# Attention one: the ring of products as two double banks in place of four banks, its reads 1024 columns wide, the layer norm's statistics in four parts

## The chip, the cores and the metric

The kernel runs on one core of a Trainium2 chip. The metric is the device time of the whole program in microseconds, lower is better. Time before: 3014.7 us, the median of 3 runs (3010.32 to 3017.59).

## The reference, cut to what matters

The program is a small language model tower of two layers on 8 sequences of 1024 tokens and width 256. The change touches the first attention only:

```python
h = W.T[tokens]                                   # (8, 1024, 256)
xh = layernorm(h).reshape(b, c, 16, 16).transpose(0, 2, 1, 3)
qkv = einsum('bhce,ef->bhcf', xh, Wqkv) + bqkv    # 16 heads of 16
q, k, v = split(qkv, 3, axis=-1)
att = einsum('bhqe,bhke->bhqk', q, k) / sqrt(16)
att = softmax(att * tril(ones((c, c)), k=-1))     # masked scores are 0, not -inf
out = einsum('bhqk,bhke->bhqe', att, v)
h = h + out.transpose(0, 2, 1, 3).reshape(b, c, d) @ Wr + br
```

A masked score counts as 0 in the softmax, so each row also needs a sum of later values of V (the suffix sums), scaled by the row's maximum.

## The kernel before, in words

**Units of work.** A sequence has 8 tiles of 128 tokens. A half (hb, 16 in all) is one sequence with 8 of its 16 heads; a group is 4 heads, so a half has two groups and the program 32. The code works in windows, one a group. A window issues 36 score slots (`S`): each fills one of 3 score banks in PSUM with 512 columns of K times Q, ACT turns it into exponentials (L554), POOL masks the diagonal blocks (L476), and PE sums them with V into `pv` in six bursts (`PV`, L717).

**The other work.** `window()` (L146) lays every other job at a slot of the window, from the positions in `AT` (L137). All engines walk the same list of events in the same order, each doing its part, with semaphores between them. gi = 0 is the window with the prologue of the next half (statistics, normalising, transposes, Q, K, V), gi = 1 the one without. `sections` runs "init" (prologue alone, then maxima), "first" (the two windows of half 0), a hardware loop over 14 halves ("loop"), "last" and "final". In the positions of `ALONE` a job has no scores beside it.

**The ring.** All products except scores and `pv` share the banks of `ring`, four of 512 fp32 columns. Each use takes the next bank; before it PE waits in `bank_free` (L338) until the use four before was read. The uses are: `XT`, transposes of the normalised tiles, read by ACT; `QK`, the products Q and K in halves of 512 tokens, read twice by ACT (L571, L572), then split into three bf16 parts by POOL and ACT (L488, L580, L493); `V`, read by DVE; `SUF`, the suffix sums; `PT`, transposes of `pv`; `OT` and `WR`, the output projection; `MX`, the scores of the next group with a mask, of which DVE takes maxima (L643); and `CT`, a transpose of 32 columns of the maxima, which a DMA carries into the stack that scores read. PE fills the two MX banks of a pair of heads together and DVE reads them one by one. The two uses of `MX` of a step are 18 steps a window, spread from slot 1 or 2 to 32.

**The layer norm.** `LN_STATS` (slot 1 of gi = 0) makes the statistics of all 8 tiles on DVE (L611, L615), `LN_NORM` (slot 3) has POOL compute (variance + eps) to the power -0.5 (L482, L484) and DVE normalise all 8 tiles (L620). MX uses are at slots 2 and 3, in this order on DVE:

```python
at(pos_of["LN_STATS"], ("LN_STATS",))
at(pos_of["LN_NORM"], ("LN_NORM",))
at(pos_of["XT"], ("R", "XT", "act", 0), ("R", "XT", "act", 1))
```

## Time and profile before

| | us |
|---|---|
| profiled execution, in all | 3005.22 |
| its span | 3002.8 |
| median of the runs | 3014.7 |
| PE busy | 2581.3 (86%) |
| DVE busy | 2118.6 (71%) |
| ACT busy | 1523.5 (51%) |
| POOL busy | 1640.4 (55%) |

The span is what the profiler recorded from the first to the last instruction. The first attention is its first half, to about 1520 us; the rest is experts, second attention and feed-forward. PE is the tensor engine's matmuls, PEld its weight loads beside them, DVE the vector engine, ACT the scalar engine, POOL GpSimd. "ring<-Km,Qm" means that an instruction writes the tile `ring` and reads `Km` and `Qm`. A bracket with an arrow gives the idle time of an engine before an instruction and whose instruction ended it. The granted clock of the tensor engine has mean 0.928 over the span, as a share of 2.4 GHz.

### The profile page before, as it was taken

Reading aid. Unit: us, or ns where it says so; the run is one execution under the profiler, and the core shown is the slowest. Engines: PE = TensorE matmul, PEld = TensorE weight load, DVE = VectorE, ACT = ScalarE, POOL = GpSimd, SP = SyncE. Lnnn points to the kernel's source line nnn. Section 1 sums busy time; section 2 is a strip of 40 time slices with the busy share of each in tenths; the row PEclk is TensorE's granted clock in tenths of the full one; section 3 lists DMA queues with packets and bytes.
Section 4 is the critical chain, followed back from the end, with each engine's and each line's share of the span. In section 5 each row is a group of like instructions: output and inputs, shape, how many; then the busy total and the mean of one; then the engine's idle time right before and its main releaser. Section 6 shows DMA issues by size and latency. Waiting matters only on the chain. (4 is left out here: it accounts for less than half of the span.)

```text
span 3002.8 us, 58475 instructions
## 1 busy us (share of the span) xinstructions
PE 2581.3 (86%) x15254; PEld 1510.3 (50%) x15318; DVE 2118.6 (71%) x5668; ACT 1523.5 (51%) x3246; POOL 1640.4 (55%) x2564
## 2 busy tenths in 40 slices
PE   1778988888988888888868999898998979999999
PEld 0323433333333333343345666666666647666666
DVE  2657766777766767676567999898888965556554
ACT  1345555555555655555513655555555634444444
POOL 3664343333334333334245877777776757777675
PEclk7679999999999999999969999999999979999999
DMA  3353343344343344334230000000000000000000
GB/s 56 89 116 62 52 63 54 52 70 69 51 63 56 53 59 70 58 54 63 36 137 1 1 1 1 1 1 1 1 1 1 1 3 16 16 14 16 16 16 18
DMA packets 81300, 113.27 MB, mean 38 GB/s; under 512 B 25100, under 2 KB 37144, under 8 KB 80536
## 3 DMA queue, kind: packets, MB, share of 16 engines
q1 hardware_dynamic: 76360, 101.44, 19.8%
q0 software_dynamic: 3072, 8.39, 1.0%
q10 hardware_dynamic: 1744, 2.16, 0.2%
q14 instruction: 92, 0.75, 0.1%
q8 instruction: 32, 0.52, 0.1%
HBM read 18.98 MB, written 8.39 MB: 9 GB/s over the span
## 5 line engine op out<-in xcount | busy, mean ns | idle before, releaser
L554 ACT ACTIVATE probs<-scoresT 128x512 f32<-128x512 f32 x1152 | 639.7, 604 | 632.4 <-PE scoresT L697 622.9
L643 DVE TENSOR_REDUCE cand<-ring 128x4 f32<-128x512 f32 x1152 | 724.1, 680 | 219.6 <-PE ring L753 167.3
L476 POOL TENSOR_SCALAR_AFFINE_SELECT probs<-probs 128x256 f32<-128x256 f32 x512 | 204.9, 414 | 468.5 <-ACT probs L554 462.4
L697 PE MATMUL scoresT<-stage 98*128 98x512 bf16 (+3 forms) x1536 | 410.3, 344 | 22.2 <-ACT probs L554 16.6
L753 PE MATMUL ring<-Km,Qm 64*128 64x512 bf16 (+2 forms) x1792 | 253.0, 321 | 160.5 <-DVE cand L643 130.5
L717 PE MATMUL pv<-probs,Vg 128*32 128x512 f32 (+3 forms) x3072 | 325.2, 545 | 28.3 <-POOL probs L476 25.9
L753 PEld LDWEIGHTS ring<-Km,Qm 64*128 64x128 bf16 x1792 | 83.5, 95 | 375.6 <-DVE cand L643 239.5
L1180 PE MATMUL mm<-w_W,hT 128*128 128x256 f32 x1024 | 259.1, 399 | 8.7 <-ACT z L1268 2.8
L1200 PE MATMUL mm<-w_W,x2T 128*128 128x512 f32 x512 | 242.4, 596 | 0.3 <-DVE x L1419 0.2
L697 PEld LDWEIGHTS scoresT<-stage 98*128 98x128 bf16 x1536 | 114.5, 99 | 234.4 <-issue 139.1
L1261 ACT ACTIVATE hT<-mmT,w_be,w_g 128x128 f32<-128x128 f32 x512 | 185.5, 469 | 90.7 <-PE mmT L1191 90.7
L1180 PEld LDWEIGHTS mm<-w_W,hT 128*128 128x128 f32 x1024 | 207.1, 202 | 36.4 <-issue 0.3
L1622 PE MATMUL down_ps<-q_down,turned 128*128 128x256 f32 (+1 forms) x768 | 201.5, 396 | 2.3 <-ACT turned L1652 2.3
L1676 POOL TENSOR_TENSOR val<-val,power 128x960 f32<-128x960 f32 (+2 forms) x68 | 129.0, 1898 | 113.0 <-ACT power L1663 113.0
L717 PEld LDWEIGHTS pv<-probs,Vg 128*32 128x32 f32 x3072 | 85.5, 115 | 191.9 <-issue 154.7
L1584 PE MATMUL gate<-q_w_gate,turned 128*128 128x352 f32 x512 | 174.0, 462 | 0.7 <-ACT turned L1647 0.5
L1584 PE MATMUL up<-q_w_up,turned 128*128 128x352 f32 x512 | 173.0, 460 | 0.0
L1622 PEld LDWEIGHTS down_ps<-q_down,turned 128*128 128x128 f32 (+1 forms) x768 | 134.9, 189 | 68.2 <-issue 43.4
L1635 ACT ACTIVATE act_g<-gate 128x352 f32<-128x352 f32 x128 | 59.3, 463 | 208.9 <-PE gate L1584 202.5
L1328 POOL TENSOR_TENSOR u<-z,w_g 128x512 f32<-128x512 f32 x128 | 160.2, 1272 | 1.7 <-ACT z L1268 1.7
L1268 ACT ACTIVATE z<-mm,nmw,rw 128x256 f32<-128x256 f32 x256 | 124.0, 571 | 48.1 <-POOL nmw L1345 47.8
L1200 PEld LDWEIGHTS mm<-w_W,x2T 128*128 128x128 f32 x512 | 98.2, 192 | 87.5 <-issue 83.3
(254 smaller groups left out, 5280.9 us busy)
## 6 DMA issues: line engine op xcount, KB each, us to landing
stage<-parts SPq DMA_DIRECT2D x256, 96.0 KB, 2.8
stage<-parts SPq DMA_DIRECT2D x256, 64.0 KB, 2.8
Qm<-parts SPq DMA_DIRECT2D x128, 128.0 KB, 2.6
Km<-parts SPq DMA_DIRECT2D x128, 128.0 KB, 2.7
stage<-parts SPq DMA_DIRECT2D x256, 32.0 KB, 2.4
out<-result SPq DMA_DIRECT2D x64, 128.0 KB, 1.7
stage<-ct SPq DMA_DIRECT2D x128, 4.0 KB
w_W<-in_W SPq DMA_DIRECT2D x4, 512.0 KB
```

The lines of the kernel that those rows point to most:

```text
L476: nc.gpsimd.affine_select(out=d, in_=d, compare_op=ALU.is_gt, fill=0.0, base=0, pattern=[[0, 2], [1, P]], channel_multiplier=-1).then_inc( ...
L554: nc.scalar.activation(probs[:, buffer(slot), :], scoresT[slot % SCORE_BANKS][:], ACT.Exp, scale=SOFT).then_inc(exp_ok, 1)
L643: ins = nc.vector.tensor_reduce(c, src[:].rearrange("p (t a b) -> p t a b", t=c.shape[1], b=P), AX.X, ALU.max)
L697: ins = nc.tensor.matmul(scoresT[slot % SCORE_BANKS][:, at:at + hi - lo], Ks[0:ROWS, gi, hh, P * kt:P * kt + P], Qs[0:ROWS, gi, hh, lo:hi] ...
L717: ins = nc.tensor.matmul(pv[32 * hh:32 * hh + 32, lo:512], Vg[:, par, kt, hh, :], probs[:, buffer(slot), column:column + 512 - lo], start= ...
L753: ins = nc.tensor.matmul(out[x][:, P * at:P * (at + n)], Qm[half[x], hh // 2, P * i:P * i + P], Km[half[x], hh // 2, P * j:P * (j + n)], s ...
L1180: ins = nc.tensor.matmul(o, hT[:, 2 * e + c, :], w["W2"][:, c, e, :], start=False, stop=(e % 2 == 1 and c == 1))
L1200: ins = nc.tensor.matmul(mm1[p][:], x2T[same][:, c, :], w["W1"][:, c, 2 * p:2 * p + 2, :].rearrange("p e n -> p (e n)"), start=False, stop ...
L1261: nc.scalar.activation(hT[:, j, :], mmT[p][:, P * k:P * k + P], ACT.Relu, bias=w["be1"][:, j:j + 1], scale=w["g1"][:, j:j + 1]).then_inc(h ...
L1328: nc.gpsimd.tensor_tensor(u[same][:, 2 * p:2 * p + 2, :], z[same][:, 2 * p:2 * p + 2, :], w["g2"][:].rearrange("p (e n) -> p e n", e=E4)[: ...
L1584: ins = nc.tensor.matmul(out[:, 0:HALF], turned[par][:, 5 + c, :], wt[:, c, HALF * a:HALF * a + HALF], start=(c == 0), stop=(c == 1))
L1622: ins = nc.tensor.matmul(down[:, 0:D], turned[1 - u][0:rows, at, :], w["down"][0:rows, k, :], start=(n == 0), stop=(n == CHUNKS - 1))
```

## The change

The ring has two double banks of 1024 columns in place of four of 512, and each use fills one whole and is read by one instruction: both heads of an MX pair, all 8 tiles of `XT`, `V`, `SUF`, `PT` and `OT`, 1024 tokens of Q or of K, 4 tiles of `WR`. The buffer `f32part` is one of 1024 columns in place of two of 512. The statistics are made in four parts at slots 0, 2, 4 and 6, POOL's power is an event of its own (`LN_POWER`, slot 6), and the normalising has four parts at slots 10 to 13. `XT` moves from slot 7 to 14, `QK` from (11, 13, 18, 20) to (16, 22), `V` from 21 to 24, `OT` from 24 to 26, `PT` from 5 and 7 to 7, `RSUM` from 5 to 3, `SUF` from 12 to 9, `WR` from slots 1 and 2 of gi = 1 to 2 and 8, and the first MX of gi = 0 from slot 2 to 1. The diff, cut to its core (the parts left out are the same steps in the waits' counts and in SP's and POOL's code):

```diff
-SCORE_BANKS, RING_BANKS = 3, 4
+SCORE_BANKS, RING_BANKS = 3, 2
 PROBS = 16
+LN_PARTS = 4
+LN_TILES = TPB // LN_PARTS
...
 AT = {
-    0: {"LN_STATS": 1, "LN_NORM": 3, "XT": 7, "PV_COPY": 4, "EQ": 6, "TMP": 0, "PT": 5, "OT": 24, "WR": 25, "RSUM": 5, "SUF": 12, "QK": (11, 13, 18, 20), "MID_LAG": 2, "V": 21, "VG": 5, "LOAD": 0, "MX": 2, "MX_END": 32, "MX_CURVE": 1.0, "PV_HALF": 14},
-    1: {"PV_COPY": 4, "EQ": 6, "TMP": 0, "PT": 5, "WR": 1, "V": 8, "VG": 6, "LOAD": 0, "MX": 1, "MX_END": 32, "MX_CURVE": 1.0, "PV_HALF": 14},
+    0: {"LN_STATS": (0, 2, 4, 6), "LN_NORM": (10, 11, 12, 13), "XT": 14, "PV_COPY": 4, "EQ": 6, "TMP": 0, "PT": 7, "OT": 26, "WR": 27, "RSUM": 3, "SUF": 9, "QK": (16, 22), "MID_LAG": 2, "V": 24, "VG": 5, "LOAD": 0, "MX": 1, "MX_END": 32, "MX_CURVE": 1.0, "PV_HALF": 14},
+    1: {"PV_COPY": 4, "EQ": 6, "TMP": 0, "PT": 7, "WR": 2, "V": 8, "VG": 6, "LOAD": 0, "MX": 1, "MX_END": 32, "MX_CURVE": 1.0, "PV_HALF": 14},
     "V_IN": 0, "WR_IN": 1,
 }
-ALONE = {"LN_STATS": 0, "LN_NORM": 1, "XT": 2, "QK": (8, 9, 10, 11), "MID_LAG": 1, "V": 12, "PV_COPY": 1, "TMP": 2, "PT": 5, "OT": 11,
+ALONE = {"LN_STATS": (0, 0, 0, 0), "LN_NORM": (1, 1, 1, 1), "XT": 2, "QK": (8, 10), "MID_LAG": 1, "V": 12, "PV_COPY": 1, "TMP": 2, "PT": 5, "OT": 11,
          "WR": 14, "VG": 14, "LOAD": 14, "MX": 15, "MX_END": 35, "MX_CURVE": 1.0}
...
 
     if prologue:
-        at(pos_of["LN_STATS"], ("LN_STATS",))
-        at(pos_of["LN_NORM"], ("LN_NORM",))
-        at(pos_of["XT"], ("R", "XT", "act", 0), ("R", "XT", "act", 1))
+        for n in range(LN_PARTS):
+            at(pos_of["LN_STATS"][n], ("LN_STATS", n))
+            at(pos_of["LN_NORM"][n], ("LN_NORM", n))
+        at(pos_of["LN_STATS"][-1], ("LN_POWER",))
+        at(pos_of["XT"], ("R", "XT", "act"))
     if tail:
         at(0, ("PV", -1, 4))
         at(3 if scores else 0, ("PV", -1, 5))
         at(pos_of["PV_COPY"], ("PV_COPY", -1, 1))
         at(pos_of["TMP"], ("TMP", -1))
-        at(pos_of["PT"], ("R", "PT", "dve", -1, 0))
-        at(pos_of["PT"] + 2, ("R", "PT", "dve", -1, 1), ("OM", -1))
+        at(pos_of["PT"], ("R", "PT", "dve", -1), ("OM", -1))
     if ot:
-        at(pos_of["OT"], ("R", "OT", "act", 0), ("R", "OT", "act", 1))
+        at(pos_of["OT"], ("R", "OT", "act"))
     if wr:
-        for j in range(4):
-            at(pos_of["WR"] + (j // 2 if scores else 0), ("R", "WR", "dve", j))
+        for j in range(2):
+            at(pos_of["WR"] + (6 * j if scores else 0), ("R", "WR", "dve", j))
     if gi == 0 and scores:
         at(pos_of["RSUM"], ("RSUM",))
-        at(pos_of["SUF"], ("R", "SUF", "dve", 0), ("R", "SUF", "dve", 1))
+        at(pos_of["SUF"], ("R", "SUF", "dve"))
     if prologue:
-        for n in range(4):
-            at(pos_of["QK"][n], ("R", "QK", "act", n // 2, n % 2))
-            at(pos_of["QK"][n] + pos_of["MID_LAG"], ("MID", n // 2, n % 2))
+        for w in range(2):
+            at(pos_of["QK"][w], ("R", "QK", "act", w))
+            at(pos_of["QK"][w] + pos_of["MID_LAG"], ("MID", w))
     if v:
-        at(pos_of["V"], ("R", "V", "dve", 0), ("R", "V", "dve", 1))
+        at(pos_of["V"], ("R", "V", "dve"))
     if following:
...
-                uses.append([("R", "MX", "dve", 2 * p, k), ("R", "MX", "dve", 2 * p + 1, k)])
+                uses.append([("R", "MX", "dve", p, k)])
...
-        f32part = sb("f32part", [P, 2, 512])
+        f32part = sb("f32part", [P, S])
...
-        ring = [ctx.enter_context(nc.psum_tensor(f"ring{i}", [P, 512], F32)) for i in range(RING_BANKS)]
+        ring = [ctx.enter_context(nc.psum_tensor(f"ring{i}", [P, S], F32)) for i in range(RING_BANKS)]
...
-                        elif kind == "LN_NORM":
-                            wait_apart(pool, (mv_ok, hb + 2))
+                        elif kind == "LN_POWER":
+                            wait_apart(pool, (mv_ok, LN_PARTS * (hb + 2)))
                             nc.gpsimd.tensor_scalar(rstd[:], mv[:, :, 1], EPS, None, ALU.add).then_inc(rs_c, 1)
                             pool.wait_ge(rs_c, hb + 2)
                             nc.gpsimd.tensor_tensor(rstd[:], rstd[:], minus_half[:], ALU.pow).then_inc(rstd_ok, 1)
                         elif kind == "R" and e[2] == "QK":
-                            w, c = e[4:6]
+                            w = e[4]
                             read(pool, section, num, e)
-                            nc.gpsimd.tensor_tensor(f32part[:, c, :], f32part[:, c, :],
-                                                    parts[:, w, 0, 512 * c:512 * c + 512], ALU.subtract).then_inc(rest_ok, 1)
+                            nc.gpsimd.tensor_tensor(f32part[:], f32part[:], parts[:, w, 0, :], ALU.subtract).then_inc(rest_ok, 1)
                         elif kind == "MID":
-                            w, c = e[2:4]
-                            pool.wait_ge(mid_ok, 4 * (hb + 1) + 2 * w + c + 1)
-                            nc.gpsimd.tensor_tensor(parts[:, w, 2, 512 * c:512 * c + 512], f32part[:, c, :],
-                                                    parts[:, w, 1, 512 * c:512 * c + 512], ALU.subtract).then_inc(parts_ok, 1)
+                            w = e[2]
+                            pool.wait_ge(mid_ok, 2 * (hb + 1) + w + 1)
+                            nc.gpsimd.tensor_tensor(parts[:, w, 2, :], f32part[:], parts[:, w, 1, :], ALU.subtract).then_inc(parts_ok, 1)
...
                             elif e[2] == "QK":
-                                w, c = e[4:6]
...
-                                    act.wait_ge(w_in, 16 * WEIGHTS)
-                                    for s in (k_in if w else q_in):
-                                        wait(act, s, 16 * 12 * (hb + 1))
-                                    for s in max_in:
-                                        wait(act, s, 16 * 4 * 2 * (hb + 1))
-                                wait(act, parts_ok, 4 * (hb + 1) + 2 * w + c - 1)
-                                nc.scalar.activation(f32part[:, c, :], src[:], ACT.Identity, bias=b_q[:, w:w + 1])
-                                nc.scalar.activation(parts[:, w, 0, 512 * c:512 * c + 512], src[:], ACT.Identity,
+                                w = e[4]
+                                act.wait_ge(w_in, 16 * WEIGHTS)
+                                for s in (k_in if w else q_in):
+                                    wait(act, s, 16 * 12 * (hb + 1))
+                                for s in max_in:
+                                    wait(act, s, 16 * 4 * 2 * (hb + 1))
+                                wait(act, parts_ok, 2 * (hb + 1) + w)
+                                nc.scalar.activation(f32part[:], src[:], ACT.Identity, bias=b_q[:, w:w + 1])
+                                nc.scalar.activation(parts[:, w, 0, :], src[:], ACT.Identity,
                                                      bias=b_q[:, w:w + 1]).then_inc(read_act, 1)
...
+                            for t in part:
                                 ins = nc.vector.bn_stats(st[:, t, :], h[:, TPB * (hn // 2) + t, :])
                             ins.then_inc(stats_c, 1)
-                            wait_apart(dve, (stats_c, hn + 1))
-                            for t in range(TPB):
+                            wait_apart(dve, (stats_c, LN_PARTS * hn + e[2] + 1))
+                            for t in part:
                                 ins = nc.vector.bn_aggr(mv[:, t, :], st[:, t, :])
                             ins.then_inc(mv_ok, 1)
                         elif kind == "LN_NORM":
                             dve.wait_ge(rstd_ok, hn + 1)
-                            for t in range(TPB):
+                            for t in range(LN_TILES * e[2], LN_TILES * e[2] + LN_TILES):
                                 nc.vector.tensor_scalar(xn[:, t, :], h[:, TPB * (hn // 2) + t, bass.ds(P * (hn % 2), P)],
                                                         mv[:, t, 0:1], rstd[:, t:t + 1], ALU.subtract, ALU.mult).then_inc(xn_ok, 1)
...
                             if e[2] == "MX":
-                                hh, k = e[4:6]
+                                p, k = e[4:6]
                                 if k == 0:
-                                    wait(dve, m_ok, PAIRS_MX * g + hh // 2)
+                                    wait(dve, m_ok, PAIRS_MX * g + p)
                                 tiles, cols = MAX_PLAN[k][2]
-                                c = cand[:, hh % 2, tiles, cols]
-                                ins = nc.vector.tensor_reduce(
-                                    c, src[:].rearrange("p (t a b) -> p t a b", t=c.shape[1], b=P), AX.X, ALU.max)
-                                ins.then_inc(read_dve, 1)
+                                c = cand[:, :, tiles, cols]
+                                nc.vector.tensor_reduce(
+                                    c, src[:].rearrange("p (i t a b) -> p i t a b", i=2, t=c.shape[2], b=P),
...
+                                wait(dve, o_ok, G - 1)
+                                nc.vector.tensor_tensor(acc[:], src[:].rearrange("p (t h e) -> p t h e", t=TPB, h=HPG)[:, :, :, 0:HE + 1],
+                                                        tmp[:], ALU.add).then_inc(read_dve, 1)
                                 read(dve, section, num, e)
-                                nc.vector.reciprocal(rden[:, t, :], acc[:, t, :, HE]).then_inc(rd_ok, 1)
+                                nc.vector.reciprocal(rden[:], acc[:, :, :, HE]).then_inc(rd_ok, 1)
...
                         elif kind == "R" and e[2] == "MX":
-                            hh, k = e[4:6]
-                            if hh % 2:
-                                continue
-                            pair = e, [x for x in plans[section] if x[:4] == e[:4] and x[4:6] == (hh + 1, k)][0]
+                            p, k = e[4:6]
                             if k == 0:
-                                pe.wait_ge(max_in[hh // 2], 16 * 4 * (g + 1))
-                            for x in pair:
-                                bank_free(pe, section, num, x)
-                            out = [ring[x[-1][0] % RING_BANKS] for x in pair]
...
-                                for t in range(4 * e[4], 4 * e[4] + 4):
+                                for t in range(TPB):
                                     pe.wait_ge(xn_ok, TPB * (hb + 1) + t + 1)
-                                    ins = nc.tensor.transpose(out[:, P * (t % 4):P * (t % 4) + P], xn[:, t, :], ident[:])
+                                    ins = nc.tensor.transpose(out[:, P * t:P * t + P], xn[:, t, :], ident[:])
                             elif e[2] == "QK":
-                                w, c = e[4:6]
-                                read(pe, section, num, use(section, "XT", c))
-                                ins = nc.tensor.matmul(out[:], w_qkv[:, w, :], xT[:, 512 * c:512 * c + 512], start=True, stop=True)
+                                read(pe, section, num, use(section, "XT"))
+                                for c in range(2):
+                                    half = slice(512 * c, 512 * c + 512)
+                                    ins = nc.tensor.matmul(out[:, half], w_qkv[:, e[4], :], xT[:, half], start=True, stop=True)
...
                                                           c12[:, nxt, 2 * e[4]:2 * e[4] + 2].rearrange("p h c t -> p (h c t)"), ident_b[:])
                             elif e[2] == "PT":
-                                pe.wait_ge(pvS_ok, 2 * (G - 1) + e[5] + 1)
-                                for t in range(4 * e[5], 4 * e[5] + 4):
-                                    ins = nc.tensor.transpose(out[:, P * (t % 4):P * (t % 4) + P], pvS[:, P * t:P * t + P], ident[:])
+                                pe.wait_ge(pvS_ok, 2 * G)
```

## Rows read from the trace of the kernel before

**Rows 1.** Busy by window; columns: us, PE, PEld, DVE, ACT, POOL, PEclk.

```profile
650.70:740.10 89.40, 76.98 (x586) 34.00 (x585) 62.01 (x122) 50.14 (x94) 33.69 (x67) 0.92 0.39 59
...
644.70:696.80 52.10, 43.45 (x324) 20.22 (x328) 34.30 (x72) 29.95 (x56) 24.03 (x43) 0.90 0.33 51
```

**Rows 2.** PE's waits in that iteration: total us, times, longest.

```profile
PE ring L753 <- DVE cand L643: 8.2, 5, 5.7
...
PE ring L739 <- ACT parts L572: 0.5, 1, 0.5
PE ring L786 <- DVE cand L643: 0.3, 1, 0.3
```

**Rows 3.** Timeline of PE, long waits: start, us, what, idle before.

```profile
214.90 0.61 PE L753 MATMUL ring<-Km,Qm 64*128 64x512 bf16 x2 [6.21 <-DVE cand L643]
...
657.05 0.61 PE L753 MATMUL ring<-Km,Qm 64*128 64x512 bf16 x2 [5.75 <-DVE cand L643]
...
1367.00 0.61 PE L753 MATMUL ring<-Km,Qm 64*128 64x512 bf16 x2 [5.74 <-DVE cand L643]
```

**Rows 4.** Timeline of DVE around the norm.

```profile
644.21 2.71 DVE L611 BATCH_NORM_STATS2 st<-h 128x6 f32 x8 [0.47 <-issue]
647.03 0.64 DVE L615 BATCH_NORM_AGGREGATE mv<-st 128x2 f32<-128x6 f32 x8
648.71 1.29 DVE L643 TENSOR_REDUCE cand<-ring 128x4 f32<-128x512 f32 x2 [1.04 <-PE ring L753]
652.62 3.77 DVE L620 TENSOR_SCALAR xn<-h,mv,rstd 128x128 f32 x8 [2.62 <-POOL rstd L484]
...
658.16 0.43 DVE L628 COPY Vg<-Vh 128x512 f32<-128x512 f32 x1
```

**Rows 5.** Busy by window: the wait, and twice 6 us after.

```profile
651.30:657.00 5.70, 0.00 (x1) 0.00 (x0) 4.38 (x10) 0.96 (x2) 4.47 (x9) 0.90 0.81 101
657.00:663.00 6.00, 5.95 (x26) 3.42 (x26) 4.49 (x10) 2.99 (x6) 2.02 (x4) 0.52 0.74 91
663.00:669.00 6.00, 6.00 (x57) 3.00 (x56) 2.56 (x5) 3.54 (x6) 1.37 (x3) 1.00 0.00 0
```

**Rows 6.** Timeline of DVE: reduces of 144 and of 512 columns.

```profile
628.65 0.30 DVE L633 TENSOR_REDUCE m<-cand 128x16 f32<-128x144 f32 x1
628.99 3.68 DVE L643 TENSOR_REDUCE cand<-ring 128x4 f32<-128x512 f32 x6
```

**Rows 7.** Timeline of POOL: the power and the suffix sums.

```profile
650.66 1.68 POOL L484 TENSOR_TENSOR rstd<-rstd,minus_half 128x8 f32<-128x8 f32 x1
...
653.20 3.11 POOL L501 TENSOR_TENSOR Rsum<-Rsum,Vh 128x128 f32<-128x128 f32 x6
```

**Rows 8.** Timeline of PE: XT, a score, a PV burst, SUF.

```profile
658.41 1.92 PE L767 MATMUL ring<-ident,xn 128*128 128x128 f32 x8
...
666.54 0.38 PE L697 MATMUL scoresT<-stage 98*128 98x512 bf16 x1
666.85 0.86 PE L717 MATMUL pv<-probs,Vg 128*32 128x256 f32 x16
667.64 0.49 PE L781 MATMUL ring<-Vh,upper 128*128 128x128 f32 x2
...
671.19 0.28 PE L753 MATMUL ring<-Km,Qm 64*128 64x256 bf16 x2
```

**Rows 9.** Timeline of ACT and POOL: QK's reads, a subtraction.

```profile
667.10 0.69 ACT L571 ACTIVATE f32part<-ring,b_q 128x512 f32<-128x512 f32 x1 [0.62 <-PE ring L771]
667.68 0.68 ACT L572 ACTIVATE parts<-ring,b_q 128x512 bf16<-128x512 f32 x1
...
668.45 1.16 POOL L488 TENSOR_TENSOR f32part<-f32part,parts 128x512 f32<-128x512 f32 x1 [4.15 <-ACT parts L572]
```

**Rows 10.** Timeline of PE, waits of the window without the norm.

```profile
709.75 0.39 PE L753 MATMUL ring<-Km,Qm 64*128 64x512 bf16 x2 [0.87 <-DVE cand L643]
...
725.03 0.39 PE L753 MATMUL ring<-Km,Qm 64*128 64x512 bf16 x2 [0.34 <-DVE cand L643]
```

103 lines of the change are left out of this document (48 added, 55 removed).

## The prediction

> **What bounds the kernel now.** I read the whole-iteration window first. One loop iteration (two windows of 36 score slots) takes 89.4 us, of which PE is busy 77.0, DVE 62.0, ACT 50.1 and POOL 33.7 [rows 1]. PE is nearest to full, with 12.4 us idle, and its queue carries scores, products and maxima in one fixed order, so a time saved elsewhere counts only if it shortens PE's list or its waits. The waits of that iteration then say whom PE waits for: DVE's reduce before a maximum matmul, 8.2 us in 5 waits, one of them 5.7, and beside it some small ones [rows 2]. The timeline of PE places the long one: once an iteration, 5.74 to 6.21 us, 14 times from the loop's first iteration on (first, one in the middle and last are shown) [rows 3]. The window with a norm that runs once, in front of the loop, has such a wait too.
>
> Its cause stands in DVE's timeline. The statistics of all eight tiles run in a block (2.71 + 0.64 us), one pair of reduces follows, then DVE waits 2.62 us for POOL's power and normalises all eight tiles in 3.77 us [rows 4]. The pair that frees the two next ring banks is queued behind that until 656.3, and PE comes back at 657.05. The windows around it show a second price: in the 5.7 us PE does nothing, and in the 6.0 us after them the granted clock is 0.52, so close to the lower level of 1.2 GHz throughout; only after 663 is it 1.00 again [rows 5]. At half speed some 2.9 of those 6.0 us are lost. The stall costs nearly 9 us an iteration, not 6.
>
> **What the change removes and adds.** First DVE's instructions. Six reduces of 512 columns in a row take 3.68 us and one record is 0.68, so they start each 0.60 us; the reduce of 144 columns takes 0.30 against 0.68, which is 1.03 ns a column [rows 6]. One reduce of 1024 thus costs DVE 0.60 + 0.53 = 1.13 us in place of 1.20. With 36 a loop iteration, and the same for the merged copies and additions (SUF, V, PT, WR), DVE has about 3 us less in 62. The work comes in the same order with the same PE matmuls, so this is worth nothing by itself: it only shortens waits on DVE, and sits in the stalls below. The Trainium skill (Perfetto Trace Analysis, Optimizing Scalar/DVE Operations) puts a DVE instruction's access overhead on PSUM at about 125 ns and says that grouping helps if the engine is saturated. The rows give 70 ns for what a merged pair saves. By the page's figure the 36 pairs would free 2 us more of DVE, an estimate, and here DVE is not saturated.
>
> Second, the layer norm. Four parts of statistics at slots 0, 2, 4 and 6 cost DVE 0.85 us each, and the four of the normalising, at 10 to 13, 0.94 each. The power (POOL, at slot 6) has four slots, some 5 us, until it is asked for; its 1.7 us fit, and the suffix sums of 3.5 us in front of it start at slot 3 [rows 7]. So the 5.75 us stall goes. With it I take out, to count the changed window afresh, what else PE waits for there: 0.40 on reduces (the other 2.05 of the 8.2 lie in the window without the norm), 0.5 on ACT's parts and 0.3 before the transposed maxima [rows 2]. That is 6.95 us. Of the clock's 2.9 I count 2.6 as back, since some shorter waits will remain together. The clock's price is bounded by 0 and 2.9.
>
> What is late next? I followed the order of the changed window with the lengths of these rows: scores 0.3 to 0.4 a slot, a maximum use 0.4 to 0.5, the short PV burst 0.8, XT 1.7 to 1.9, SUF 3.55 from its first matmul to the next product's [rows 8]. With two double banks a product waits until the use two before it has been read whole. Five places come out late:
> - Slots 1 to 7. From the first filled maximum, DVE has 4 reduces (4.5), three parts of statistics (2.9) and Vg (0.43), 7.8 us, ahead of the read that frees the bank of the sixth ring use. PE reaches it after 5.9. Stall 1.9.
> - XT, now at 14. From the end of SUF's 3.55 us fill, DVE has SUF's read (1.2), two reduces (2.3) and the four normalisings (3.8), 7.3 us; PE has 4.3 us of work. Of the 3.0 late, 1.5 is covered as each transposition waits for its own tile alone. Stall 1.5.
> - The maximum behind XT: its bank's reduce is queued behind the normalising. Stall 0.9.
> - The first QK. ACT reads a half twice at a pitch of 0.58 [rows 9], so both halves twice in about 2.1 us, all in one use. PE has a maximum and two score slots (1.2) before it asks for the bank again. Stall 0.9.
> - The second QK at 22: the transposed maxima, at 23, take its bank. PE has some 0.9 against 2.1. Stall 1.2.
> Together 6.4 us. None of these waits is in the trace as such. The lower bound is 2 us, if DVE and ACT keep ahead at all but two places; the upper is 10, if each of these five and the long reads of SUF, V, OT and WR show by 1 us or so, the pair's read of 1.2 us being the measure. I stay near the walk.
>
> What QK does to its own chain: POOL's subtractions become 2 x 1.16 each [rows 9], so POOL and ACT hand over in 2.1 + 2.3 + 1.1 + 2.3 = 7.8 us a product, with one buffer. ACT will wait about 1.3 us at the middle part, which three score banks cover, and the last part is done some 9 slots before the next window loads it. If that cover is gone, the price is up to 2 us an iteration, inside the 10 above.
>
> Third, the window without the norm. PE waits there for reduces (0.87 at 709.75 after the second PT, 0.34 at 725.03 after the transposed maxima [rows 10]). With one PT the first shrinks by about 0.4. The second grows by a reduce's half, 0.5: the small product of the transposed maxima now blocks a double bank, and the maximum behind it waits for the whole of the one before it, where it waited for half. Sum +0.1, between -1 and +2.
>
> **Sum.** An iteration changes by -6.95 - 2.6 + 6.4 + 0.1 = -3.05 us. Fifteen windows have the norm beside scores: -46. Before the loop, the first Q and K have nothing beside them: two rounds of 7.8 us with one buffer in place of four shorter ones that overlap, +3 (0 to 8); the end, with the last PT, OT and WR alone, +1. Together -42. The profiled execution has 3002.8 span and 3005.2 in all, 2.4 around it that the change doesn't touch; it would become 2963. The median of the runs, 3014.7, is 9.5 higher than the profiled one, and the difference goes to it: 2973. With the bounds: new stalls of 2, all of the clock and the gain of the other window give -8.9 an iteration, -130 in all; stalls of 10, no clock and +2 there give +5, +80.
>
> **The rivals.**
> (a) Full gain, 0.2. Both the stall and the low clock go and the five places cost about 3 us. For it: PE and DVE are not each other's limit over a window (43.5 and 34.3 us of the window's 52.1 [rows 1]), and my walk stacks each delay without letting later waits shrink. Against it: in slots 1 to 14 DVE has as much work as PE. -6.95 - 2.9 + 3 + 0.1 = -6.75, times 15, +4: -97, 2918.
> (b) The ring is too coarse, slower, 0.2. The mechanism: each non-maximum use holds half of all ring space from its first matmul to the end of one long read, so PE, with only one other bank, stops at QK, SUF, V, OT and WR. It decides from new stalls of 9.3 us an iteration on; at 11, without more than 2.6 of clock, -6.95 - 2.6 + 11 + 0.1 = +1.55, times 15, +4: +27, 3042. For it: a PE wait on a DVE read is already the largest, with four banks. Against it: the maxima, 36 of some 50 uses, took banks in pairs before, and for them nothing gets coarser. The Trainium skill (Perfetto Trace Analysis, Matmuls) wants independent groups rotated through different PSUM banks, so that one's evacuation overlaps the next one's matmuls. The change keeps that for two groups only; by that rule this rival is the one to expect.
> (c) The long stall only moves, 0.1. The power is queued on POOL behind the suffix sums (slot 3) and the masks; if it ends 3 us after slot 10, DVE stands at the first normalising with the reduces behind it, as now. Then 3 us join the 6.4: -6.95 - 2.6 + 9.4 + 0.1 = about 0 if three waits of 3 us leave the clock alone, +2.5 if they don't. With the first, 3015 + 4 = 3019. Against it: four slots are about 5 us.
>
> **How the numbers follow.** The forecast holds 0.5 with its own range 2945 to 3000. Faster by over 0.2% (6 us, about what can be told from no change): all of (a) and nearly all of the forecast, 0.70. Within 0.2%: a part of (c) and of the forecast's upper end, 0.07. Slower: (b), a part of (c), 0.23. The range reaches down past (a)'s value and up to where (b) begins, 2905 to 3028.
>
> **What would show it.** The reduce's record should be about 1.21 us with 576 of them; no wait of PE on a reduce above 3 us once the loop runs; granted clock near 1.00 where the iteration has 657 to 663 now; new rows of PE behind ACT's parts (about 2 us an iteration) and behind normalised tiles (1.5). The iteration should be near 86.3 us. The prediction is wrong if the waits of PE on DVE and ACT sum to under 4 or over 10 us in the window with the norm, if the clock stays low after short waits, or if PE's busy time changes by itself.

## The result, and the profile after

The changed kernel takes 3032.12 us (median of 5 runs, 3031.0 to 3036.71) against 3013.06 us before (5 runs beside them): ratio 1.0065, interval 1.005 to 1.008. It is slower by 0.65%, and the forecast of 2973 with its range up to 3028 was wrong. The profiled execution took 3036.71 us, span 3034.7.

The 31.9 us of span between the two traces split into four parts. Up to the end of the first attention +64.4 us (1514.1 to 1578.5); the weights' preparation behind it +9.3; the experts' loop, whose code is unchanged, **-43.4**; all behind it +1.6. So in these traces the attention lost twice what the span shows, and something unforeseen paid most of it back. Between POOL's powers of the loop's iterations the period went from 88.63 to 92.24 us. Windows of the changed kernel (columns as in [rows 1]): two iterations, the part with the norm, and three stretches of 4 us in it.

```profile
785.80:970.07 184.27, 156.05 (x1172) 68.54 (x1172) 115.40 (x157) 99.14 (x172) 65.58 (x122) 0.93 0.38 57
773.70:829.90 56.20, 47.15 (x320) 21.25 (x320) 31.53 (x50) 28.67 (x47) 22.58 (x37) 0.85 0.30 45
805.70:809.70 4.00, 2.58 (x18) 0.81 (x22) 2.58 (x3) 2.74 (x5) 2.13 (x1) 0.81 0.00 0
809.70:813.70 4.00, 4.00 (x22) 1.07 (x15) 1.27 (x2) 2.83 (x5) 2.13 (x1) 0.76 0.00 0
817.70:821.70 4.00, 4.00 (x25) 2.79 (x24) 1.53 (x2) 2.19 (x3) 2.83 (x2) 0.59 0.00 0
```

The same over two iterations of before, and its experts' loop:

```profile
740.36:918.29 177.93, 152.67 (x1174) 67.85 (x1173) 124.26 (x244) 100.38 (x189) 67.65 (x134) 0.92 0.39 59
1611.80:2411.90 800.10, 722.83 (x3311) 526.91 (x3373) 716.47 (x2856) 445.92 (x1249) 591.79 (x1115) 0.97 0.00 1
```

Twelve iterations, before and then after:

```profile
295.83:1360.64 1064.81, 913.83 (x7033) 406.48 (x7032) 745.10 (x1464) 602.15 (x1128) 406.03 (x805) 0.93 0.39 59
```

```profile
324.55:1430.50 1105.95, 936.41 (x7032) 411.31 (x7032) 692.68 (x937) 594.91 (x1032) 393.71 (x733) 0.93 0.37 57
```

Per iteration PE's idle time is (1105.95 - 936.41) / 12 = 14.1 against 12.6, and its busy time 78.0 against 76.2 for the same matmuls: both rose, by 1.5 and 1.9. The window with the norm has granted clock 0.85, against 0.90 in [rows 1]. PE's waits in the two iterations of after shown first (columns as in [rows 2]) show the 5.7 us wait gone, and one name grown:

```profile
PE ring L741 <- DVE cand L639: 6.1, 10, 1.1
PE ring L780 <- DVE cand L639: 3.8, 4, 1.5
PE ring L775 <- ACT parts L569: 3.5, 2, 1.8
PE ring L741 <- ACT parts L569: 3.4, 2, 1.7
...
PE pv L709 <- POOL probs L479: 2.1, 4, 0.8
...
PE ring L755 <- DVE cand L639: 1.3, 2, 0.7
```

PE's timeline of after places them:

```profile
802.69 1.88 PE L760 MATMUL ring<-xT,w_qkv 128*128 128x512 f32 x4
804.50 0.39 PE L741 MATMUL ring<-Km,Qm 64*128 64x512 bf16 x2
804.82 0.60 PE L689 MATMUL scoresT<-stage 98*128 98x512 bf16 x2
807.12 0.39 PE L741 MATMUL ring<-Km,Qm 64*128 64x512 bf16 x2 [1.70 <-ACT parts L569]
...
808.74 3.33 PE L709 MATMUL pv<-probs,Vg 128*32 128x512 f32 x16
...
817.05 0.23 PE L775 MATMUL ring<-ident_b,c 128*32 128x128 bf16 x1 [1.76 <-ACT parts L569]
...
817.44 2.69 PE L763 MATMUL ring<-w_qkv,xT 128*128 128x128 f32 x16
```

and ACT's timeline says why:

```profile
804.95 1.11 ACT L568 ACTIVATE f32part<-ring,b_q 128x1024 f32<-128x1024 f32 x1 [1.19 <-PE ring L741]
805.96 1.11 ACT L569 ACTIVATE parts<-ring,b_q 128x1024 bf16<-128x1024 f32 x1
```

The first QK is done at 804.6. ACT reads its double bank twice and ends at 807.07. Only one use of the ring and two scores stand between, so PE waits 1.70 us. Soon after, a PV burst runs in 3.33 us, at or near the lower level of the clock (granted clock 0.57 from 808.74 to 812.07); such a burst takes 1.7 to 1.9 where the clock is full. The second QK repeats it: 1.76 us, then V in 2.69. The merged reduces are as forecast: 576 of 1215 ns. The page of after shows them, and above them the packets of the queue that it calls instruction, which matter further down:

```profile
q14 instruction: 36, 0.29, 0.0%
...
L639 DVE TENSOR_REDUCE cand<-ring 128x8 f32<-128x1024 f32 x576 | 688.4, 1215 | 367.3 <-PE ring L741 297.8
```

**The experts' loop.** Before, DVE stands still eleven times in it, twice each time, with nothing that the profile could name as releaser. Waits of before, 1611.8 to 2411.9:

```profile
DVE gy L1378 <- issue: 27.3, 11, 2.6
DVE both L1382 <- issue: 23.1, 11, 2.3
```

One of the eleven, timeline of DVE before:

```profile
1832.68 0.41 DVE L1490 TENSOR_TENSOR h<-sum_ps,h 128x256 f32 x1
1835.57 0.16 DVE L1378 SCALAR_TENSOR_TENSOR gy<-rank,gx 128x4 f32<-128x4 f32 x1 [2.48 <-issue]
1837.83 1.89 DVE L1382 TENSOR_REDUCE both<-u 128x256 f32<-128x1024 f32 x1 [2.10 <-issue]
```

That is 4.6 us a time, 50 us in all; after has none of them. The page of before has 92 packets where after has 36:

```profile
q14 instruction: 92, 0.75, 0.1%
```

DVE's part of this loop is 306 instructions; it begins as DVE's 1219th before and its 1026th after, since the merged reads shortened the attention's code (counted in the programs; no view of a trace shows these places). The Trainium skill (Runtime: NRT & Kernel Launch, Instruction fetch mechanics) says that a taken branch whose target is outside what the engine holds stalls until it is fetched. The idle rows and the packets agree with that. e1 and e2 test the place, though not the fetch by itself.

### The profile page after: what moved, and what is told of

Read it like the earlier page. It is cut to its first block and busy times, and to the rows that moved or that the text cites. A ratio compares the mean times of both kernels' runs of the same rounds, so it can differ in the third digit from the quotient of the medians.

```text
span 3034.7 us, 55799 instructions
## 1 busy us (share of the span) xinstructions
PE 2595.2 (86%) x15254; PEld 1500.6 (49%) x15318; DVE 2068.2 (68%) x4964; ACT 1514.9 (50%) x3118; POOL 1629.2 (54%) x2468
## 5 line engine op out<-in xcount | busy, mean ns | idle before, releaser
L639 DVE TENSOR_REDUCE cand<-ring 128x8 f32<-128x1024 f32 x576 | 688.4, 1215 | 367.3 <-PE ring L741 297.8
L709 PE MATMUL pv<-probs,Vg 128*32 128x512 f32 (+3 forms) x3072 | 339.4, 566 | 33.5 <-POOL probs L479 24.1
L1169 PE MATMUL mm<-w_W,hT 128*128 128x256 f32 x1024 | 243.4, 381 | 8.3 <-ACT z L1257 3.1
L513 POOL CAST c<-m 128x16 bf16<-128x16 f32 x64 | 12.7, 198 | 398.5 <-DVE m L629 398.5
L1169 PEld LDWEIGHTS mm<-w_W,hT 128*128 128x128 f32 x1024 | 195.8, 191 | 31.1
L1611 PEld LDWEIGHTS down_ps<-q_down,turned 128*128 128x128 f32 (+1 forms) x768 | 134.9, 189 | 68.2 <-issue 43.4
```

Source lines behind the costliest of these rows:

```text
L639: nc.vector.tensor_reduce(c, src[:].rearrange("p (i t a b) -> p i t a b", i=2, t=c.shape[2], b=P), AX.X, ALU.max).then_inc(read_dve, 1)
L709: ins = nc.tensor.matmul(pv[32 * hh:32 * hh + 32, lo:512], Vg[:, par, kt, hh, :], probs[:, buffer(slot), column:column + 512 - lo], start= ...
L1169: ins = nc.tensor.matmul(o, hT[:, 2 * e + c, :], w["W2"][:, c, e, :], start=False, stop=(e % 2 == 1 and c == 1))
L1611: ins = nc.tensor.matmul(down[:, 0:D], turned[1 - u][0:rows, at, :], w["down"][0:rows, k, :], start=(n == 0), stop=(n == CHUNKS - 1))
```

## The experiments

A wait for a semaphore that has its value already (a met wait) serves as padding. "Period" is the mean time between POOL's powers in the loop (13 of them), "attention" its end, "experts" the length of their loop, each from the run's trace. Times of different sections come from different sets of runs, each with its own runs of before beside it: the ratio is to those.

**e1_after_shift.** The changed kernel, DVE's code shifted by 193 instructions:

```diff
                 sections(dve, run)
+                for _ in range(386):
+                    dve.wait_ge(const_ok, 3)
```

> Changed kernel with 386 waits that are already met behind the vector engine's part of the first attention; they take 193 instructions, so the loop over experts starts at instruction 1219 of DVE, where the kernel before has it (1026 in the changed kernel). Theory 'code position': the changed kernel gained some 43 us in the loop over experts only because DVE's loop (306 instructions) lies elsewhere in the code; here the stalls of DVE before L1378 and L1382 of the kernel before (11 of each, about 4.6 us a pair) come back, that loop takes 800 us instead of 757, and the total is about 3032 + 43 = 3075. Rival 'phase': the difference comes from the state in which the attention leaves queues and clock; then this kernel stays within 5 us (plus at most 5 us for the waits themselves) of 3032.

3093.62 us, ratio 1.0275 (1.0258 to 1.0292). Period 92.21, experts 802.8: with the loop's start at 1219 again (1026 + 193) its stalls are back: eleven, 46 us, with 92 packets. Another 16.5 us lie between attention and experts, so the total is above the 3075 expected. They are the padding itself, which is not free: before its next instruction DVE stands 18.51 us here, 0.40 in the changed kernel and 6.42 in e2, some 47 ns for each added wait.

```profile
1609.31 0.27 DVE L949 MEMSET v_w_gate<- 64x256 f32 x1 [18.51 <-PEq L360]
```

**e2_before_shift.** Before, with 127 such waits (63 instructions).

2973.12 us, ratio 0.9875 (0.9858 to 0.9891). Period 88.61, experts 757.1 against 800.1. With nothing but met waits added, the old kernel is faster than before and than the changed kernel. By its place alone the loop costs 43 to 46 us. No other run but before and e1 has the stalls: all the rest have 35 to 38 packets on that queue and an experts' loop of 754 to 757 us. The fair comparison of the two attentions is this run with the changed kernel: 59 us apart, with 6 us of padding in e2. One trace tells the attention's end only to some 5 us: the same attention code ended at 1514.1 in before and 1518.5 here, and at 1578.5 in the changed kernel and 1573.5 in e1.

**e3_norm_alone.** Before's ring of four banks, with the norm in four parts at the new slots:

```diff
-"LN_STATS": 1, "LN_NORM": 3, "XT": 7, "SUF": 12, "QK": (11, 13, 18, 20), "V": 21, "OT": 24
+"LN_STATS": (0, 2, 4, 6), "LN_NORM": (10, 11, 12, 13), "XT": 14, "SUF": 9, "QK": (16, 17, 20, 22), "V": 24, "OT": 26
```

> Kernel before, ring of four banks and half reads kept, with the norm in parts and its products at the changed kernel's slots (statistics 0, 2, 4, 6; normalising 10 to 13; XT 14; QK 16, 17, 20, 22; V 24; OT 26; RSUM 3; SUF 9; first maxima 1). Theory A (the coarse ring costs what the norm gains): the iteration goes from 88.6 us to 84 to 86, PE's wait of 5.7 us is gone and no other one over 2 us comes, since a half is free after half the read; at the ring's price the changed kernel is then 6 to 8 us an iteration worse than this. Theory B (the norm's new place is itself what costs: DVE has too much in slots 0 to 14 and the short waits put the clock low while PE works): 90 to 92 us, near the changed kernel's 92.2. The total follows with 14 or 15 iterations, if the loop over experts keeps its 800 us.

3006.16 us, ratio 0.9987 (0.9977 to 0.9997). Period 91.41, experts 753.9, which alone keeps the total under that of before. The new places cost 2.8 us an iteration with four banks too. PE's waits on ACT's parts are there as well: 4.8 us over two iterations, against 1.1 before and 6.9 in the changed kernel.

**e8_ring_alone.** The other half: double banks, norm in one pass, before's slots (`LN_PARTS = 1`, XT 7, QK 11 and 18, SUF 12, V 21, OT 24, WR 25 and 1).

> Changed kernel's ring and reads, with the norm in one part at the slots of the kernel before (statistics 1, norm 3, XT 7, SUF 12, QK 11 and 18, V 21, OT 24, first maxima 2). From the kernel with the norm alone (91.4) and the changed one (92.2) the ring is worth +0.8. Theory 'the two parts add': 88.6 + 0.8 = 89.4, with the wait of 5.7 us back. Rival 'the ring is the main cost and the parts of the norm hide it': 92 or more. If DVE's merged reads are worth more than the coarser ring: below 88.6.

2977.02 us, ratio 0.9893 (0.9876 to 0.9909). Period 88.63, experts 754.6, under the 89.4 that adding the two parts had given. At before's slots the coarse ring costs nothing; at the new ones it costs 0.8 (92.24 against e3's 91.41). So rival (b), that the ring is too coarse, is not the main cause, and the Trainium skill's rule cited with it (Perfetto Trace Analysis, Matmuls) had no price at before's slots.

**e4_short_qk.** The changed kernel; in the loop ACT reads 64 of QK's 1024 columns. The kernel leaves out the rest of Q and K, so its output is no longer that of the reference; it serves for timing alone:

```diff
-nc.scalar.activation(f32part[:], src[:], ACT.Identity, bias=b_q[:, w:w + 1])
+n = S if section == "init" else 64
+nc.scalar.activation(f32part[:, 0:n], src[:, 0:n], ACT.Identity, bias=b_q[:, w:w + 1])
...
```

> Changed kernel; after the first prologue ACT reads only 64 of the 1024 columns of each QK product (both reads), so most of Q and K is not renewed. What it takes away is PE's two waits for ACT's long reads (1.70 before the maxima, 1.76 before the transposed maxima at 807 and 817 us of the profile). Theory 'clock': the stretches at the lower level right after those waits (807.7 to 811.5 and 817.7 to 822, or 893 to 896) go with them, so the iteration falls by 3.4 us of waits plus 2 to 3.5 us of busy time, from 92.2 to about 86. Rival 'waits only': the clock is low for another reason and the iteration falls by 3.4 to 88.8. Rival 'something else is late then' (DVE's reduces or POOL's subtraction): it falls by less than 2.

2989.46 us, ratio 0.9916 (0.9897 to 0.9935). Period 89.46, 2.8 us less: short of what both theories of the expectation gave (86 and 88.8). ACT's long reads of two products, on an engine that is half idle, cost 2.8 us an iteration where they stood.

**e5_fill.** The changed kernel with redundant score matmuls of the next slot ahead of six waits:

```diff
+FILL = {("PT", 7): 4, ("MX", 7): 1, ("XT", 14): 1, ("MX", 14): 2, ("MX", 18): 4, ("CT", 23): 4}
```

> Changed kernel; in the loop's window with the norm PE makes the next slot's scores some times over, just ahead of six of its waits (4 times before PT, 1 before the maxima of slot 7, 1 before XT, 2 before the maxima of slot 14, 4 before those of slot 18, 4 before the transposed maxima of slot 23), into a score bank that is its own at that time; 0.3 us each at the full clock, so about as long as the waits were. The last real product overwrites them. Theory 'clock' (the short waits put the clock at its lower level, which then holds for the 3 to 6 us of work behind them): the waits shrink by what is filled, the stretches at 0.50 after 784, 807 and 817 us go, and the iteration falls from 92.2 to 88 to 90. Rival 'the clock follows something else' : the clock stays, the extra products cost their own time where they are longer than the wait, and the iteration is 92.2 to 95.

3009.91 us, ratio 0.9997 (0.9987 to 1.0007). Period 90.48, just above the 88 to 90 expected; granted clock of two iterations 0.97. PE makes the scores of 16 slots more an iteration and is 1.8 us sooner: the low clock behind these waits has a price, about half of the +3.6.

**e6_late_maxima.** `"MX_CURVE": 0.75` in place of 1.0, to take maxima away from the norm's slots.

> Changed kernel with the maxima of the window with the norm bent to later slots (curve 0.75 in place of 1: slots 1, 4, 6, 9, 11, 12 up to 13 in place of 1, 2, 4, 6, 7, 9, 11, 13). Theory 'DVE is the limit from slot 0 to 14 and the norm's new place fills it': two reduces less there (2.3 us) shorten PE's waits by 1.5 to 2.5 us an iteration and some low clock with them, 92.2 to about 89.5. Rival 'the reads of the ring are the limit wherever they lie': the waits come back in slots 15 to 35, where the maxima are now denser, 92 to 93.

3085.37 us, ratio 1.0247 (1.023 to 1.0264), period 95.60. A miss: my view that DVE's load around the norm sets the pace falls. **e7_norm_late_maxima**, the same curve on e3's kernel, took 3023.45 us (ratio 1.0037, 1.0023 to 1.0051) with period 92.14, where 88.5 to 89.5 was expected from that view: a second miss.

**e9_before_shift_fill and e10_ring_alone_fill** put redundant scores into the one long wait, of e2 (18 at slot 5) and of e8 (15 at slot 7):

```diff
+if section == "loop" and gi == 0 and e[1:3] == ("R", "XT"):
+    wait(pe, exp_ok, UNITS * G + nslot + 1 - SCORE_BANKS)
+    for _ in range(15):
...
```

> The version before with its code shifted (127 met waits on VectorE after attention one, as in the shifted version of before that measured 2973.12 us), and in the loop, ahead of the maxima's products of slot 5 in the window with the norm, 18 redundant score matmuls of slot 6 (about 0.30 us each, 5.4 us) inside the wait of 5.75 us [rows 3]. They leave the waited-for event where it is. Clock theory (the clock falls to 0.52 in the 6 us after the long wait [rows 5], and this was the term of -2.6 us per iteration in the prediction): the granted clock stays high through 657:663, the products behind the wait go about 3 us faster, and the loop period of 88.61 falls to about 86, the kernel to about 2935 us (2930 to 2950). Rival (the iteration is set by VectorE or by ScalarE's exponentials right behind the wait, so PE's faster work there is only waited off again): clock high, period 88.3 to 88.7, kernel 2968 to 2978. Rival 2 (the added products overshoot the wait): period above 89, kernel above 2980.

> The changed kernel's ring of double banks with the norm where it was before (one pass, slots of before), which measured 2977.02 us with a period of 88.63 us, and in the loop, ahead of the transposes XT at slot 7, 15 redundant score matmuls of slot 8 (about 0.30 us each, 4.5 us) inside its wait of 4.8 us. Clock theory: the low-clock stretch behind the wait goes, the period falls by 2 to 3 us to about 86, the kernel to about 2940 us (2932 to 2955). Rival (VectorE or ScalarE sets the iteration behind the wait): 2972 to 2980. The difference to the version with before's ring and the same filling tells whether the coarse ring costs anything once the clock is full: by the ring theory (every use holds two banks) it would be slower than that one by 1 us or more per iteration, by the theory so far (ring costs nothing) within 10 us of it.

2969.35 (0.9879, 0.9862 to 0.9895; period 88.71) and 2971.11 us (0.9887, 0.987 to 0.9903; period 88.78). The clock did rise in e10, yet no period fell: both expectations by the clock (86) missed. The clock behind the long wait, which the prediction had counted as 2.6 us, is worth nothing in these two orders, where the wait itself stays. In e9 the filling ran in 4.1 us and 2.0 of wait were left, so e10 is the clean one. Windows of e8, then of e10: two iterations, 4 us behind the long wait, and 4 us that start 28 us later.

```profile
481.22:658.38 177.16, 149.91 (x1180) 67.51 (x1172) 117.39 (x157) 97.57 (x173) 65.42 (x123) 0.95 0.39 60
...
664.00:668.00 4.00, 2.82 (x13) 2.78 (x14) 2.66 (x3) 0.82 (x1) 1.72 (x4) 0.50 0.83 102
...
692.00:696.00 4.00, 2.21 (x14) 1.14 (x13) 3.30 (x4) 1.91 (x4) 2.06 (x1) 1.00 0.12 22
```

```profile
476.35:653.81 177.46, 155.60 (x1240) 71.63 (x1232) 117.46 (x157) 97.89 (x173) 65.41 (x123) 0.97 0.39 60
...
660.00:664.00 4.00, 2.85 (x20) 1.99 (x20) 2.65 (x4) 1.02 (x1) 1.23 (x3) 1.00 0.85 104
...
688.00:692.00 4.00, 3.08 (x13) 2.02 (x15) 1.53 (x3) 1.13 (x2) 0.29 (x1) 0.67 0.48 110
```

The same three waits, in PE's timeline of e8 and then of e10:

```profile
692.98 0.39 PE L741 MATMUL ring<-Km,Qm 64*128 64x512 bf16 x2 [0.46 <-DVE Vh L647]
694.20 0.22 PE L775 MATMUL ring<-ident_b,c 128*32 128x128 bf16 x1 [0.83 <-DVE cand L639]
...
695.24 1.09 PE L784 MATMUL ring<-ident,O 128*128 128x128 f32 x8 [0.49 <-DVE cand L639]
```

```profile
687.21 0.39 PE L751 MATMUL ring<-Km,Qm 64*128 64x512 bf16 x2 [0.46 <-DVE Vh L647]
688.43 0.23 PE L785 MATMUL ring<-ident_b,c 128*32 128x128 bf16 x1 [0.83 <-DVE cand L639]
...
689.46 1.97 PE L794 MATMUL ring<-ident,O 128*128 128x128 f32 x8 [0.49 <-DVE cand L639]
```

Equal waits, one with full clock behind it and one with half. Counted from its norm's power, e10 reaches these transposes 1.2 us earlier than e8 (35.65 against 36.86 us), and they take 0.9 longer.

**e11_late_gathers.** The changed kernel; POOL's gathers of "first" 12 slots later (`0 <= gi * UNITS + slot - 12 < TILES - TPB`).

> The changed kernel with the 56 gathers of the remaining token rows issued from GpSimd 12 slots later in the first pair of windows (slots 12 to 67 in place of 0 to 55). Queue theory for the 8.2 us wait of PE at 116.9 us (the mask of probs is behind gathers, suffix sums and the norm's power on GpSimd): that wait shrinks by 4 to 7 us, the attention ends 4 to 7 us earlier (about 1572.5), the kernel takes about 3026 us. Rival (the wait comes from GpSimd's suffix sums and the power alone): under 2 us of change, 3030 to 3034. The loop period stays 92.2 under both.

3026.66 us, ratio 1.0066 (1.0049 to 1.0083), period 92.22. The wait of 8.21 us fell to 2.73, so in the first window POOL's queue held a mask behind gathers, suffix sums and power. What that is worth in all is not shown: the attention ends at 1572.6, 5.9 sooner than in the changed kernel's trace but only 0.9 sooner than in e1, whose attention is the same code, and the ratio is the changed kernel's own (1.0065).

**e12_parts_early.** The changed kernel, norm's parts at 6, 6, 7, 7, XT 9, QK 13 and 18, SUF 12, V 21, OT 24.

> The changed kernel with the norm still in four parts, but early: statistics at slots 0, 1, 2, 3, the norm's parts at 6, 6, 7, 7, XT at 9 (not 14), QK at 13 and 18 (not 16 and 22), V 21, OT 24, WR 25, suffix sums 12, maxima from 2, as before's placement. Crowding theory (the +3.6 us per iteration of the changed kernel come from the seven uses from XT on being pressed between slots 14 and 28, each with its read): period 88 to 89, the kernel at 2965 to 2985 us. Parts theory (the split itself costs, by its added waits of VectorE between products and reads): period stays at 91 to 92.5, 3015 to 3035 us. The second clock question: with XT's wait cut from 4.8 us to under 3 us, a period below 88.3 would say that the long wait had a price in the ring-alone version; the fillings have shown 88.7 and 88.8, so by them it stays at 88.6.

3032.97 us, ratio 1.0049 (1.0033 to 1.0066), period 92.24: the crowding theory falls, as far as this placement tests it, since it brings a wait of 3.8 us of its own. Waits of two iterations:

```profile
PE ring L741 <- DVE acc L656: 7.6, 2, 3.8
PE ring L727 <- ACT parts L569: 3.2, 2, 1.6
```

**e13_split_in_place, e14_whole_late.** e8 with the four parts all at slots 1 and 3; and the changed kernel with one pass, statistics at 6, norm at 12.

> The ring-alone version (double banks, before's slots; 2977.02 us, period 88.63) with one change: statistics and norm in four parts, but all four at the slots of the one pass (statistics 1, norm 3). Split theory (the four parts themselves cost, as 1.0 us of VectorE's own short waits and the added waits of GpSimd): period 91 to 92.5, kernel 3010 to 3030. Placement theory: period 88.5 to 89, kernel 2974 to 2984, since VectorE only gets three more pairs of short waits in the norm's 8 us.

> The changed kernel with the norm in one pass again, at the new late places (statistics at slot 6, norm at slot 12, all else as changed: XT 14, QK 16 and 22, V 24, OT 26, WR 27). Split theory: period 88.5 to 89.5, as the split is gone. Placement theory: period 92 or above (92 to 94: the late place costs, and the one pass of 3.9 us holds VectorE at a stretch before XT's), kernel 3030 to 3060.

2977.21 us (0.9881, 0.9864 to 0.9897), period 88.75; and 3073.19 us (1.0201, 1.0184 to 1.0218), period 95.34. The split is free; in the late place it even helps by 3.1 us. That leaves the order of the uses. Where e8 and e13 have QK, suffix sums, maxima in the ring, the changed kernel and e12 have QK, maxima, maxima: nothing long covers ACT's two reads.

**e15_suf_behind.** The changed kernel with that order restored by moving two events:

```diff
-"SUF": 9, "QK": (16, 22)
+"SUF": 18, "QK": (17, 22)
```

> The changed kernel with the suffix sums' two banks of products at slot 18 in place of 9, and the first QK at slot 17 in place of 16, so that the ring's order is QK, suffix sums, maxima. Cover theory: the wait of 1.7 us on ScalarE's parts behind the first QK goes, and with it part of the low clock behind it: period from 92.24 to 89 to 90.7, kernel at 2990 to 3010 us. Rival (it is the late place as such, the norm's work on VectorE colliding with more maxima): period 92 or more, as the suffix sums now add to the crowded end, 3030 to 3050.

2981.0 us, ratio 0.9894 (0.9877 to 0.991). Period 89.09, 3.15 us less an iteration, and 51 us less in all than the changed kernel's median, a little better than the 2990 to 3010 expected. Its windows (two iterations; behind the suffix sums) and PE's timeline:

```profile
498.83:676.40 177.57, 152.35 (x1172) 68.00 (x1172) 115.49 (x157) 99.38 (x172) 65.65 (x123) 0.94 0.38 59
785.00:789.00 4.00, 3.44 (x25) 0.84 (x23) 3.10 (x3) 2.20 (x4) 2.72 (x2) 1.00 0.00 0
```

```profile
779.03 1.98 PE L760 MATMUL ring<-xT,w_qkv 128*128 128x512 f32 x4
...
784.51 0.39 PE L741 MATMUL ring<-Km,Qm 64*128 64x512 bf16 x2
...
786.54 1.93 PE L709 MATMUL pv<-probs,Vg 128*32 128x512 f32 x16
```

No wait on ACT's parts behind the first QK (0.56 us on DVE's read of the suffix sums is left), and the PV burst in 1.93 in place of 3.33 us. The waits ahead of this QK in the window sum to 4.3 us against 4.5, so the gain does not come from the emptied slot 9. PE's idle time fell by 1.5 us an iteration ((28.22 - 25.22) / 2) and its busy time by 1.85: a wait, and as much again in the clock.

**e16_early_suf.** e12 with SUF at 14, behind its first QK at 13.

> The parts-early version (norm at 6, 6, 7, 7, XT 9, QK 13 and 18; period 92.24) with the suffix sums at slot 14 in place of 12, directly behind the first QK. Cover theory: the wait of 1.6 us on ScalarE's parts goes, period 89 to 90.7, kernel 2980 to 3010 us. Rival (the collision is on VectorE, in the wait of 3.8 us behind the accumulator): period 91.5 to 92.5.

2996.59 us, ratio 0.9942 (0.9926 to 0.9959), period 89.98: 2.3 us less. The number is in the expected range, but the mechanism expected did not happen. A maximum still stands between QK and the suffix sums, and the wait on ACT's parts only moved to the latter, 1.79 in place of 1.58 us:

```profile
685.61 1.88 PE L760 MATMUL ring<-xT,w_qkv 128*128 128x512 f32 x4
...
690.04 0.49 PE L770 MATMUL ring<-Vh,upper 128*128 128x128 f32 x2 [1.79 <-ACT parts L569]
```

Over twelve iterations PE's idle time fell by 0.7 us an iteration and its busy time by 1.6 (901.88 against 921.00 in all). So e16 shows that the order moves the time, mostly by the clock, but it does not confirm the covered wait; for that e15 and e4 stand.

**e17_both_behind.** e15 with V at 23 in place of 24, behind the second QK.

> e15 with V at slot 23 in place of 24, so that the second QK product too has a long use of the ring (V's 16 products) behind it before the maxima and the transpose CT ask for banks. Cover theory with the clock's share: the wait of 1.76 us goes and V runs in 1.7 in place of 2.6 us: period from 89.09 to 86.5 to 87.5, kernel 2945 to 2962 us. Rival one (only the wait goes, the clock falls elsewhere): period 87.3 to 88.5, 2958 to 2973. Rival two (the iteration is held at 88.6 to 89 by the long chain of VectorE, as the fillings e9 and e10 could suggest): no change, 2978 to 2984.

2976.56 us, ratio 0.9886 (0.987 to 0.9903), period 88.64. PE's timeline:

```profile
694.64 1.95 PE L763 MATMUL ring<-w_qkv,xT 128*128 128x128 f32 x16
696.80 0.39 PE L741 MATMUL ring<-Km,Qm 64*128 64x512 bf16 x2 [0.21 <-ACT parts L569]
698.00 0.22 PE L775 MATMUL ring<-ident_b,c 128*32 128x128 bf16 x1 [0.81 <-DVE Vh L647]
```

The wait shrank from 1.76 to 0.21 and V ran in 1.95 in place of 2.69, yet only 0.45 us an iteration came of it, outside all three expected ranges, between rival one and no change: 0.81 of wait moved to CT, and over twelve iterations PE's busy time did not fall (919.48 against 917.71 in e15).

## Why the prediction was wrong

**The clock term of -2.6 us an iteration failed first.** The prediction counted the low clock behind the long wait as given back. PE's busy time rose by 1.9 us instead, so this term accounts for 4.5 of the 6.65 us between the -3.05 forecast and the +3.6 measured. Eight waits of 0.35 to 1.8 us, 7.9 us together, in the place of one of 5.75 left PE at the lower level while it had work to do ([rows 5] against the windows above). The loop's mean granted clock, 0.93 in both kernels over twelve iterations, hides this, since it counts the idle stretches too. The prediction named "if the clock stays low after short waits" as what would break it. And e10 shows that even a full clock behind the long wait is worth nothing in e8's order. e5 gives the other side: filling the short waits of the changed kernel was worth 1.8 us.

**The QK stalls were mis-sized.** 0.9 and 1.2 us were forecast at the first and the second QK; 1.70 and 1.76 were measured, 1.4 us more together. I had counted ACT's reads right (2.1 against 2.12) but not the 0.4 us until ACT starts, nor how little PE has in between. By e15 the first one cost 3.15 us an iteration with what the clock added, most of the +3.6.

**Right in kind:** the 5.75 us wait went; the merged reduce takes 1.215 us (1.21). The stalls of slots 1 to 7 are 2.7 (1.9), XT's 0.7 (1.5), that of the maximum behind it 0.8 (0.9). The five places sum to 7.6 us against the 6.4 forecast. PE's idle time rose by 1.5 us an iteration, where -6.95 + 6.4 + 0.1 = -0.45 was forecast: 1.2 of these 2.0 us are at the five places, the other 0.8 was not traced. So the walk named the right places and came within a fifth of their sum, but that error and the untraced part are together as large as the gain that it was to find. The "near 86.3 us" for the iteration also started from one of 89.4, above the loop's mean of 88.63. The chain of POOL and ACT on QK's parts cost nothing visible.

**Rivals.** The outcome lies near (b)'s 3042 at 3032, and that is luck: the attention alone lost more than (b)'s +27, and the experts' loop gave 43 back. Of its mechanism the stops at QK came, but e8 has the coarse ring at 88.63 us and e3 has most of the loss with four banks. (c) did not happen: no wait on the power in the loop. (a) did not either.

**Terms outside the loop.** The loop's first exponential came 18.2 us later (219.91 against 201.65). Of these, 4.6 lie in the prologue alone (first score at 100.13 against 95.49), where +3 was forecast. The rest lies in the first two windows, where PE waits 8.21 us on POOL; before, its longest wait there was 5.35 on DVE. The experts' loop, which the forecast had no term for, gave -43. A forecast that had the attention right would have come to 3013 + 64 = 3077 and been wrong the other way.

**Open:** six versions (before, e8, e9, e10, e13, e17) all end between 88.6 and 88.8 us, with idle times of PE from 8.7 to 13.9 us. What holds them there is not shown. Nor is it shown why the new places cost 2.8 us with four banks (e3): the suffix sums were not moved behind QK there. And it is open why DVE's loop of 306 instructions stalls from place 1219 and not from 1026 or 1282: that padding switches the stalls on and off is shown, the fetch as their cause is inferred from the packets.

## What to carry to other kernels

In a ring with few buffers, look at what is issued right behind each use whose reader reads twice or late, and put the longest other use there: one such swap was worth 51 us. Taking a wait of PE out need not give its length: e17 took 1.55 us out and gained 0.45, e15 took 1.70 out and gained 3.15. Sum waits and busy time apart, and don't book the clock as gain while short waits replace the long one. When an edit changes the number of instructions ahead of a later loop, compare that loop's time first, and pad with met waits before you judge the edit (here they cost some 47 ns each).

## What the hardware showed that I had not expected

- 63 instructions of met waits on DVE, ahead of a loop, made the whole program 1.25% faster; 193 of them made the other version 2.0% slower (3093.62 against 3032.12), of which 46 us are the loop's stalls and 16.5 the padding.
- Equal waits of 0.46, 0.83 and 0.49 us were followed by full clock in one kernel and by half in another, at the same place of the order. The Trainium skill (TensorE: Matmul & The Clock Gate, What's actually happening) describes a gate whose observation runs freely, not reset by the program. The two timelines do not contradict it, but PE's work ahead of these waits differs too, so no run here shows it.
- Redundant matmuls inside waits made a kernel faster (e5, 0.7% under the changed one), with a granted clock of 0.97 over two iterations in place of 0.93. In e10 they raised it too, from 0.95 to 0.97, and gained nothing.
